# Running sums of k taken by TensorE from the k features; GpSimd's outer products cut from 1152 to 1024 columns

## The chip, the cores and the metric

The kernel runs on one core of one Trainium2 chip. The metric is device time in microseconds, the median of several executions of the same program. Engines are named as the profile names them: PE is TensorE's matmul, PEld its weight load, DVE is VectorE, ACT is ScalarE, POOL is GpSimd, SP is SyncE.

## The reference

The input is 32 x 256 tokens of 128 numbers, in fp32. Three layers follow each other: `x + 0.5 * moe(layernorm(x))`, `x + attention(layernorm(x))`, `x + 0.5 * moe(layernorm(x))`. The first and the last are the same mixture of 8 experts (two for each token) with a shared expert. The one in the middle is a linear attention whose scan runs over the 32 sequences, for each of 256 positions:

```
q, k, v = split((x @ W_attn + b_attn))          # 16 heads of 8
q, k = elu(q) + 1, elu(k) + 1
kv   = kv + k[..., :, None] * v[..., None, :]   # 8 x 8 a head
ksum = ksum + k
y    = (q . kv) / (q . ksum + 1e-6)
out  = y @ W_proj + b_proj
```

With 16 heads, `kv` has 16 x 8 x 8 = 1024 numbers a token and `ksum` has 128.

## The kernel before

Tokens are taken in 16 groups of 512 (`NG`), each of four tiles of 128 (`NJ`). The program has five phases with a barrier between them. Phase 1 is the first MoE's shared expert and routing; phase 2 its experts in blocks of 256 rows. Phase 3 (`streams`) runs, for group m, three things side by side: the attention of group m+1 and m+2, and the shared expert and the routing of the second MoE for group m-1 and m. Phase 4 is the experts of the second MoE, phase 5 the last sum and the store. The change touches phase 3 only.

Each engine has its own instruction list, written out by hand in the order in which it runs; engines wait for each other by counting semaphores. The loop of phase 3 (`streams_of`) has two groups in its body, and three groups ahead of it and four behind it are written out apart.

The attention of a group goes in two halves q = 0, 1 of two tiles a = 0, 1:

- PE makes q, k, v of a tile (`qkv_products`, into banks 3 and 4 of PSUM). ACT takes the exponential and copies v to `val` (L650, L652); DVE makes the features of q and k from them (`features`, `qk`, L1359).
- POOL makes the outer products of a tile (`outer`, L510): `kv` = k times v for each head, with k in `qk` and v in `val`. `val` has 9 columns a head, and the ninth is 1.0 (`VD = HD + 1`, written by `memset` at L547, once), so that one product of 16 x 9 x 8 = 1152 columns (`KVW`) holds k times v and k itself.
- PE turns them into running sums (`running_sums`, L945 and L947). For a = 0 it multiplies the fp32 matrix `upto` (a triangle of ones) by the 1152 columns, in three matmuls of 320, 512 and 320 columns, since a bank of PSUM ends at 512. For a = 1 each of the three is followed by a second one with `ones32` and the columns of a = 0. They lie in `PKV`, columns 192 to 1343 of banks 5 to 7. In the trace each fp32 matmul is two records, each with a weight load of its own.
- DVE multiplies the sums by q (`attend`, L1366, from PSUM to `prod`), adds eight neighbours (L1369, into `num`), and after four tiles divides (`divide`, L1374 to L1378, into `y32`). PE transposes `y32` (L957), ACT and DVE split it in two fp16 parts, and PE projects it.

The waits that the prediction speaks of: PE's `running_sums` waits for POOL's `s_outer` and for DVE's `s_sums_read` (L1366 has read the sums before). DVE's `attend` waits for `s_running_sums`. DVE's `place` (L1219, L1221, `pk` at L1223) gives each token its row in the routing table; ahead of it DVE waits for `s_running_sums` of tile (1, 0). PE's `positions` (L891, L893) waits for the `s_sums_read` of tile (0, 0) of the group after. `deviations` (L1174 to L1192) ends the norms' scale on DVE, and POOL's `outer(m + 1, 1, 0)` waits for it. `combine` (L517) adds the experts' results to X on POOL; `row_low` and `low` (L503) are fp16 remainders; `scatter` (L482, L485) sends 8 indirect DMAs a group from POOL's queue. `keep_warm` (L1055) is nine matmuls that nothing reads.

PE's list for the loop: `gate_up(0)`, `running_sums(0, 1)`, `keep_warm(9)`, `gate_up(1)`, `running_sums(1, 0)`, transposes and qkv of the next half, `running_sums(1, 1)`, transposes, qkv, `down`, `running_sums(0, 0)` of the next group, `logits`, `y_transposes`, `project`, `positions`. POOL's list: `outer(1, 0)`, `low`, `outer(1, 1)`, `combine`, `row_low`, `outer(0, 0)`, `outer(0, 1)`, `scatter`.

## Time and profile before

| | |
|---|---|
| three runs | 1367.43, 1369.38, 1383.91 us |
| median | 1369.38 us |
| profiled execution, first to last instruction | 1240.9 us |
| median less that span | 128.5 us |
| phase 3 (attention) in the profiled execution | about 460 to 947 us |
| busy over the span | PE 80%, DVE 72%, POOL 68%, ACT 54% |

The page gives the profiled execution's span and no time of its own beside it. What lies around the span (median less span) has no instruction of the program in it. A record of the trace has a start, a duration and, in square brackets, how long the engine had been idle before it and what ended that. All times in rows are microseconds from the span's start, except where a column is said to be in ns.

### The profile page before, as it was taken

The page shows a single profiled execution, that of the slowest core. Times are in us where ns is not written, and L with a number is a line of the kernel's source. Part 1 is how long each engine was busy: PE and PEld are TensorE (multiplying, and loading weights), DVE is VectorE, ACT ScalarE, POOL GpSimd, SP SyncE. Part 2 cuts the span into 40 slices and gives each one's busy share as a digit, 9 for nine tenths or more (in the row PEclk, how much of TensorE's full clock was granted, in tenths as well). Part 3 has the DMA queues.
Part 4 walks back from the last instruction along what each step waited for, and adds up shares of the span by engine and source line. Part 5 has one row for each costly group of instructions (what it writes and reads, how often), then busy time and mean ns, then how long its engine had stood idle before and what let it go on. Part 6 is the DMA issues. An engine that isn't in the chain of part 4 may idle for free. (4 is left out here: it accounts for less than half of the span.)

```text
span 1240.9 us, 31979 instructions
## 1 busy us (share of the span) xinstructions
PE 989.7 (80%) x8996; PEld 742.7 (60%) x8997; DVE 896.8 (72%) x2369; ACT 669.6 (54%) x1466; POOL 843.8 (68%) x872
## 2 busy tenths in 40 slices
PE   2657665999999927788888888888864999999940
PEld 1434344899989924455555555555543888899930
DVE  6778784676676745788888888888854666666748
ACT  4556642555555523466665656666331555555545
POOL 4677773777777845467787787778642677777750
PEclk9898996999999968999999999999966999999985
DMA  9411122222222221001111111100003222222229
GB/s 279 108 51 47 52 76 66 78 79 76 78 77 78 68 59 33 17 33 37 34 34 51 34 38 41 41 17 18 23 27 87 74 74 77 78 75 78 73 95 332
DMA packets 68607, 86.62 MB, mean 70 GB/s; under 512 B 13004, under 2 KB 56209, under 8 KB 68558
## 3 DMA queue, kind: packets, MB, share of 16 engines
q1 hardware_dynamic: 51278, 52.15, 14.5%
q0 software_dynamic: 17280, 33.87, 8.3%
q8 instruction: 25, 0.41, 0.1%
q14 instruction: 24, 0.20, 0.1%
HBM read 44.74 MB, written 43.04 MB: 71 GB/s over the span
## 5 line engine op out<-in xcount | busy, mean ns | idle before, releaser
L496 POOL DMA_INDIRECT expert_results<-ey,eidx x284 | 293.3, 1033 | 70.9 <-issue 69.6
L485 POOL DMA_INDIRECT routed_rows<-row,idx x256 | 255.2, 997 | 73.6 <-issue 70.2
L1142 DVE SCALAR_TENSOR_TENSOR ehT<-eh,ehT 128x768 f16<-128x768 f32 x142 | 136.1, 958 | 150.1 <-ACT ehT L688 150.1
L683 ACT ACTIVATE esil<-PSUM 128x768 f32<-128x768 f32 x142 | 115.1, 810 | 230.2 <-PE PSUM L826 224.6
L824 PE MATMUL PSUM<-eT,WGU 128*128 128x256 f16 x852 | 234.3, 275 | 1.4
L825 PE MATMUL PSUM<-eT,WGU 128*128 128x256 f16 x852 | 233.9, 275 | 0.0
L826 PE MATMUL PSUM<-eT,WGU 128*128 128x256 f16 x852 | 233.8, 274 | 0.0
L510 POOL TENSOR_TENSOR space<-qk,val 128x1152 f32<-128x1152 f32 x64 | 138.2, 2171 | 69.5 <-DVE shift L1192 48.7
L824 PE MATMUL PSUM<-WD,ehT 128*128 x852 | 161.0, 220 | 8.3 <-DVE ehT L1142 5.0
L825 PE MATMUL PSUM<-WD,ehT 128*128 x852 | 159.3, 220 | 0.0
L826 PE MATMUL PSUM<-WD,ehT 128*128 x852 | 158.8, 219 | 0.0
L945 PE MATMUL PSUM<-space,upto 128*128 128x320 f32 (+1 forms) x384 | 148.4, 496 | 9.6 <-DVE prod L1366 6.8
L1292 DVE SCALAR_TENSOR_TENSOR eh<-PSUM,esil 128x768 f32<-128x768 f32 x142 | 134.9, 950 | 8.1 <-ACT esil L683 8.1
L494 POOL TENSOR_TENSOR carrier<-ones 128x1 f32<-128x1 f32 x142 | 73.0, 514 | 72.6 <-ACT ey L697 72.6
L688 ACT ACTIVATE ehT<-eh 128x768 f16<-128x768 f32 x142 | 118.6, 835 | 2.5 <-DVE eh L1292 2.5
L945 PEld LDWEIGHTS PSUM<-space,upto 128*128 128x128 f32 x384 | 71.8, 193 | 59.7 <-issue 42.0
L1366 DVE TENSOR_TENSOR prod<-PSUM,qk 128x1152 f32<-128x1152 f32 x64 | 86.3, 1348 | 13.9 <-PE PSUM L947 9.3
L824 PEld LDWEIGHTS PSUM<-eT,WGU 128*128 x852 | 83.7, 98 | 18.8 <-issue 6.8
L824 PEld LDWEIGHTS PSUM<-WD,ehT 128*128 128x128 f16 x852 | 82.9, 97 | 14.3 <-issue 9.7
L1369 DVE TENSOR_REDUCE space<-prod 128x144 f32<-128x1152 f32 x64 | 86.6, 1353 | 5.8
L826 PEld LDWEIGHTS PSUM<-eT,WGU 128*128 x852 | 84.0, 99 | 10.4
L825 PEld LDWEIGHTS PSUM<-eT,WGU 128*128 x852 | 84.1, 99 | 7.3
(197 smaller groups left out, 2300.0 us busy)
## 6 DMA issues: line engine op xcount, KB each, us to landing
xe<-routed_rows SPq DMA_DIRECT2D x142, 130.0 KB, 2.1
space<-expert_results SPq DMA_DIRECT2D x32, 512.0 KB, 3.9
expert_results<-ey,eidx POOLq DMA_INDIRECT x284
X<-in_L_attn_x_dram SPq DMA_DIRECT2D x16, 256.0 KB, 4.6
routed_rows<-row,idx POOLq DMA_INDIRECT x256, 2.3
out_dram<-X SPq DMA_DIRECT2D x16, 256.0 KB, 4.3
routed_rows<-pad_rows SPq DMA_DIRECT2D x24, 130.0 KB
space<-in_L_ffn_Wg_dram SPq DMA_DIRECT2D x1, 1408.0 KB, 9.1
```

Source lines behind the costliest of these rows:

```text
L485: pool.indirect_dma_start(routed, bass.IndirectOffsetOnAxis(ap=idx[u][:, k, j:j + 1], axis=0), row[u][:, j, :], None).then_inc(s_scattered ...
L496: pool.indirect_dma_start(result, bass.IndirectOffsetOnAxis(ap=eidx[u][:, h:h + 1], axis=0), ey[u][:, h, :], None, bounds_check=K * T - 1, ...
L510: pool.tensor_tensor(kv[:, q, a, :].rearrange("p (h j i) -> p h j i", h=HEADS, j=VD), k4, v4, ALU.mult).then_inc(s_outer, 1)
L683: act.activation(esil[u][:, :], PSUM[:, 1536 * u:1536 * u + 768], ACT.Silu, scale=2.0 ** -(SX + SWT)).then_inc(s_block_silu, 1)
L688: act.activation(ehT[u][:, 0, :, :], eh32[u][:, :].rearrange("p (c t) -> p c t", c=NC), ACT.Copy).then_inc(s_block_high, 1)
L824: pe.matmul(dst, a[0], b[0], start=start, stop=False)
L825: pe.matmul(dst, a[0], b[1], start=False, stop=False)
L826: return pe.matmul(dst, a[1], b[0], start=False, stop=stop)
L945: mm = pe.matmul(PKV[:, lo:hi], upto[:, :], kv[:, q, a, lo:hi], start=True, stop=(a == 0))
L1142: return dve.scalar_tensor_tensor(out=dst, in0=src, scalar=float(2 ** scale), in1=high, op0=ALU.mult, op1=ALU.subtract)
L1292: dve.scalar_tensor_tensor(out=eh32[u][:, :], in0=PSUM[:, at:at + NC * BLK], scalar=2.0 ** (SH - SX - SWT), in1=esil[u][:, :], op0=ALU.mul ...
L1369: dve.tensor_reduce(num[:, j, :, :], prod[:, a, :].rearrange("p (h j i) -> p h j i", h=HEADS, j=VD), AX.X, ALU.add)
```

## The change

- `val` has 8 columns a head and is laid out value first: `[HD, HEADS]`, so column j * 16 + h. ACT's copy reads PSUM in steps of 8 fp32 for that and writes without gaps; before, it read without gaps and wrote 8 of each 9. The `memset` of the ones is gone.
- `outer` makes 1024 columns, `kv[j, h, i] = k[h, i] * v[j, h]`.
- `running_sums` first multiplies `upto` (and `ones32`) by the k features themselves, 128 columns of `qk`, then by the two halves of `kv`, 512 columns each. `PKV` is moved to columns 384 to 1535 of banks 5 to 7, so that each piece lies in a bank of its own: 128, 512, 512.
- `attend` reads q as nine copies of a run of 128 instead of 16 x 9 x 8; `num` is value first, with the sum of k in row 0. `divide` reads `num` in that order and writes `y32` with steps of 8 fp32.

```diff
-KVW = HEADS * HD * VD
+KW = HEADS * HD
+KVW = KW * VD
...
-        val = sb("val", [P, 2, 2, HEADS, VD])
-        kv = reused("p (q a w) -> p q a w", q=2, a=2, w=KVW)
-        num = reused("p (j h v) -> p j h v", j=NJ, h=HEADS, v=VD)
+        val = sb("val", [P, 2, 2, HD, HEADS])
+        kv = reused("p (q a w) -> p q a w", q=2, a=2, w=KW * HD)
+        num = reused("p (j v h) -> p j v h", j=NJ, v=VD, h=HEADS)
...
-        KV0 = (3 * 512 - KVW) // 2
-        PKV = bank(5, 3)[:, KV0:KV0 + KVW]
+        PKV = bank(5, 3)[:, 3 * 512 - KVW:3 * 512]
...
-                k4 = qk[:, q, a, D:2 * D].rearrange("p (h j i) -> p h j i", h=HEADS, j=1).to_broadcast([P, HEADS, VD, HD])
-                v4 = val[:, q, a, :, :].rearrange("p h (j i) -> p h j i", i=1).to_broadcast([P, HEADS, VD, HD])
-                pool.tensor_tensor(kv[:, q, a, :].rearrange("p (h j i) -> p h j i", h=HEADS, j=VD), k4, v4, ALU.mult
+                k4 = qk[:, q, a, D:2 * D].rearrange("p (j h i) -> p j h i", j=1, h=HEADS).to_broadcast([P, HD, HEADS, HD])
+                v4 = val[:, q, a, :, :].rearrange("p j (h i) -> p j h i", i=1).to_broadcast([P, HD, HEADS, HD])
+                pool.tensor_tensor(kv[:, q, a, :].rearrange("p (j h i) -> p j h i", j=HD, h=HEADS), k4, v4, ALU.mult
                                    ).then_inc(s_outer, 1)
...
-                    for q in range(2):
-                        pool.memset(val[:, q, :, :, HD:VD], 1.0)
...
-                    last = act.activation(val[:, q, a, :, 0:HD], PG[a][:, 2 * D:3 * D].rearrange("p (h j) -> p h j", h=HEADS),
+                    last = act.activation(val[:, q, a, :, :], PG[a][:, 2 * D:3 * D].rearrange("p (h j) -> p j h", h=HEADS),
...
-                for lo, hi in ((0, 512 - KV0), (512 - KV0, 1024 - KV0), (1024 - KV0, KVW)):
-                    mm = pe.matmul(PKV[:, lo:hi], upto[:, :], kv[:, q, a, lo:hi], start=True, stop=(a == 0))
+                pe.matmul(PKV[:, 0:KW], upto[:, :], qk[:, q, a, D:2 * D], start=True, stop=(a == 0))
+                if a:
+                    pe.matmul(PKV[:, 0:KW], ones32[:, :], qk[:, q, 0, D:2 * D], start=False, stop=True)
+                for lo in (0, 512):
+                    sums = PKV[:, KW + lo:KW + lo + 512]
+                    mm = pe.matmul(sums, upto[:, :], kv[:, q, a, lo:lo + 512], start=True, stop=(a == 0))
                     if a:
-                        mm = pe.matmul(PKV[:, lo:hi], ones32[:, :], kv[:, q, 0, lo:hi], start=False, stop=True)
+                        mm = pe.matmul(sums, ones32[:, :], kv[:, q, 0, lo:lo + 512], start=False, stop=True)
...
-                q4 = qk[:, q, a, 0:D].rearrange("p (h j i) -> p h j i", h=HEADS, j=1).to_broadcast([P, HEADS, VD, HD])
+                q3 = qk[:, q, a, 0:D].rearrange("p (v c) -> p v c", v=1).to_broadcast([P, VD, KW])
...
-                dve.tensor_tensor(y32[:, :, :].rearrange("p j (h i) -> p j h i", h=HEADS), num[:, :, :, 0:HD],
-                                  rden[:, :, :].rearrange("p j (h i) -> p j h i", i=1).to_broadcast([P, NJ, HEADS, HD]),
+                dve.tensor_tensor(y32[:, :, :].rearrange("p j (h i) -> p j i h", h=HEADS), num[:, :, 1:VD, :],
+                                  rden[:, :, :].rearrange("p j (i h) -> p j i h", i=1).to_broadcast([P, NJ, HD, HEADS]),
                                   ALU.mult).then_inc(s_y, 1)
```

## Rows read from the trace of the kernel before

**Rows 1.** Busy time by stretch, two groups of the loop (busy us by engine, count):

```profile
core 0: us, PE busy (x) PEld busy (x) DVE busy (x) ACT busy (x) POOL busy (x), PEclk, DMA share, GB/s
620.61:647.99 27.38, 24.01 (x151) 14.97 (x149) 23.64 (x65) 17.61 (x39) 22.37 (x18) 1.00 0.12 39
647.99:675.37 27.38, 24.02 (x147) 14.73 (x145) 24.14 (x64) 17.39 (x39) 20.87 (x18) 1.00 0.11 39
```

**Rows 2.** Records of DVE in order of time, two groups:

```profile
620.61 0.19 DVE L1219 TENSOR_TENSOR posb<-PSUM,base 128x32 f32<-128x32 f32 x1 [1.06 <-PE PSUM L945]
620.95 0.49 DVE L1223 TENSOR_TENSOR pk<-pick,posb 128x64 f32<-128x64 f32 x1
...
627.59 1.36 DVE L1366 TENSOR_TENSOR prod<-PSUM,qk 128x1152 f32<-128x1152 f32 x1 [0.18 <-PE PSUM L947]
...
635.84 1.35 DVE L1366 TENSOR_TENSOR prod<-PSUM,qk 128x1152 f32<-128x1152 f32 x1
...
647.99 0.19 DVE L1219 TENSOR_TENSOR posb<-PSUM,base 128x32 f32<-128x32 f32 x1 [1.26 <-PE PSUM L945]
...
648.33 1.13 DVE L1223 TENSOR_TENSOR pk<-pick,posb 128x64 f32<-128x64 f32 x1
...
655.40 1.33 DVE L1366 TENSOR_TENSOR prod<-PSUM,qk 128x1152 f32<-128x1152 f32 x1
...
663.72 1.34 DVE L1366 TENSOR_TENSOR prod<-PSUM,qk 128x1152 f32<-128x1152 f32 x1
...
675.37 0.19 DVE L1219 TENSOR_TENSOR posb<-PSUM,base 128x32 f32<-128x32 f32 x1 [1.06 <-PE PSUM L945]
```

**Rows 3.** Records of PE in order of time, from positions to the sums:

```profile
637.33 0.18 PE L891 MATMUL PSUM<-chosen,before 128*128 128x32 f16 x1 [0.51 <-DVE prod L1366]
...
643.12 1.51 PE L1055 MATMUL PSUM<-SGW,ident 128*128 128x352 f16 x9
...
645.76 2.10 PE L945 MATMUL PSUM<-space,upto 128*128 128x320 f32 x6
```

**Rows 4.** Records of POOL in order of time, same two groups:

```profile
619.19 2.18 POOL L510 TENSOR_TENSOR space<-qk,val 128x1152 f32<-128x1152 f32 x1
621.32 1.27 POOL L517 TENSOR_TENSOR X<-X,space 128x512 f32 x1
...
642.49 2.17 POOL L510 TENSOR_TENSOR space<-qk,val 128x1152 f32<-128x1152 f32 x1 [1.29 <-DVE shift L1192]
644.87 1.16 POOL L503 TENSOR_TENSOR xa<-xn,xa 128x512 f16<-128x512 f32 x1 [0.21 <-ACT xa L641]
645.98 2.17 POOL L510 TENSOR_TENSOR space<-qk,val 128x1152 f32<-128x1152 f32 x1
648.11 1.26 POOL L517 TENSOR_TENSOR X<-X,space 128x512 f32 x1
...
654.33 4.30 POOL L510 TENSOR_TENSOR space<-qk,val 128x1152 f32<-128x1152 f32 x2 [1.44 <-DVE qk L1359]
```

**Rows 5.** Groups by line and shape, 500 to 880 us (busy us, mean ns | idle before):

```profile
L510 POOL TENSOR_TENSOR space<-qk,val 128x1152 f32<-128x1152 f32 x56 | 121.0, 2171 | 53.1 <-DVE shift L1192 40.2 <-DVE qk L1359 12.3
L945 PEld LDWEIGHTS PSUM<-space,upto 128*128 128x128 f32 x336 | 61.9, 190 | 45.5 <-issue 30.6 <-POOL space L510 2.2
L482 POOL TENSOR_TENSOR ticket<-ones 128x1 f32<-128x1 f32 x13 | 2.5, 191 | 0.0
L1198 DVE TENSOR_REDUCE lg<-PSUM 128x32 f32<-128x64 f32 x14 | 3.0, 212 | 0.0
L1226 DVE TENSOR_REDUCE idx<-pk 128x8 uint32<-128x64 f32 x13 | 2.9, 220 | 1.4
L1378 DVE TENSOR_TENSOR space<-space,rden 128x512 f32<-128x512 f32 x14 | 9.7, 696 | 1.0
L652 ACT ACTIVATE val<-PSUM 128x128 f32<-128x128 f32 x56 | 12.2, 274 | 0.0
```

**Rows 6.** fp32 transposes of 128 columns, weight loads and matmuls:

```profile
632.83 0.42 PEld L957 LDWEIGHTS PSUM<-ident,space 128*128 128x128 f32 x4
632.83 0.66 PE L957 MATMUL PSUM<-ident,space 128*128 128x128 f32 x4
```

**Rows 7.** Records of DVE and PE ahead of the loop, behind POOL's products:

```profile
477.50 1.36 DVE L1366 TENSOR_TENSOR prod<-PSUM,qk 128x1152 f32<-128x1152 f32 x1 [0.61 <-PE PSUM L945]
...
485.39 2.20 PE L945 MATMUL PSUM<-space,upto 128*128 128x320 f32 x6 [0.93 <-POOL space L510]
...
510.39 2.20 PE L945 MATMUL PSUM<-space,upto 128*128 128x320 f32 x6 [1.82 <-POOL space L510]
```

**Rows 8.** Records of DVE's pk in other groups:

```profile
539.41 0.22 DVE L1223 TENSOR_TENSOR pk<-pick,posb 128x64 f32<-128x64 f32 x1
...
593.71 1.06 DVE L1223 TENSOR_TENSOR pk<-pick,posb 128x64 f32<-128x64 f32 x1
...
812.60 1.13 DVE L1223 TENSOR_TENSOR pk<-pick,posb 128x64 f32<-128x64 f32 x1
```

More of the change, by code:

```diff
@@ L1364, in attend @@
                 dve.wait_ge(s_running_sums, m * NJ + (j + 1))
[L1365 to L1367 removed]
+                q3 = qk[:, q, a, 0:D].rearrange("p (v c) -> p v c", v=1).to_broadcast([P, VD, KW])
+                dve.tensor_tensor(prod[:, a, :].rearrange("p (v c) -> p v c", v=VD),
+                                  PKV[:, :].rearrange("p (v c) -> p v c", v=VD), q3, ALU.mult).then_inc(s_sums_read, 1)
                 dve.drain()
[L1369 removed]
+                dve.tensor_reduce(num[:, j, :, :], prod[:, a, :].rearrange("p (v h i) -> p v h i", v=VD, h=HEADS),
                                   AX.X, ALU.add)
@@ L1373, in divide @@
                 dve.drain()
-                dve.tensor_scalar(rden[:, :, :], num[:, :, :, HD], EPS_DEN * 4.0 ** SF, None, ALU.add)
+                dve.tensor_scalar(rden[:, :, :], num[:, :, 0, :], EPS_DEN * 4.0 ** SF, None, ALU.add)
                 dve.drain()
```

3 lines of the change are left out of this document (removed).

## The prediction

> **What bounds the kernel now.** The change touches only the attention phase, so I left the chain of work that ended last aside (it shows the experts and their indirect DMAs) and read the phase as a loop. First, busy time by stretch over one group and the next [rows 1]: both take 27.38 us; PE is busy 24.0 of them, DVE 23.6 to 24.1, POOL 20.9 to 22.4. Nobody is full, PE and DVE are nearly so, and POOL, the engine that the change relieves, has 5 to 6 us to spare. A busy share says nothing about order, so next came the records of each engine in order of time. The reader is to look for the points where one engine waits for another and where that other is itself not waiting.
>
> The loop closes like this. PE finishes the sums of tile (1, 0), and DVE, which had been idle for 1.06 or 1.26 us, starts `place` at 620.61 and 647.99 [rows 2]. From there DVE works almost without a gap until it has multiplied the sums of tile (0, 0) of the next group, at 635.84 and 663.72 [rows 2]. PE waited for that, with `positions` at 637.33 [rows 3], and from there runs without a pause that another engine causes through `gate_up`, the sums of (0, 1), `keep_warm`, `gate_up` and the sums of (1, 0), which start at 645.76 and let DVE go at 647.99 [rows 2, 3]. So of 27.38 us some 10.7 are PE's (637.33 to 647.99) and 16.7 are DVE's. POOL is in neither part. Its product (1, 0) ends at 644.66, 1.1 us ahead of the PE record that needs it; its product (1, 1) ends at 648.15, when DVE, in `place`, has yet to read the sums ahead of it; its first product of the next group ends at about 656.5, halfway into the pair that starts at 654.33, and those sums come last in PE's list [rows 3, 4]. In front of the first product POOL stands idle for 1.29 us, waiting for DVE [rows 4].
>
> There is one place where POOL's length does reach the loop. DVE's `pk` (L1223), 64 elements with both inputs in SBUF, takes 0.22 us where nothing is in its way [rows 8], 0.49 us at 620.95 and 1.13 us at 648.33 [rows 2]. At 620.95 it ends at 621.44, when POOL's product does (621.37); at 648.33 it has missed the end of the product (648.15) and ends at 649.46, when POOL's `combine` does (648.11 + 1.26 = 649.37) [rows 2, 4]. So `pk` stands still while POOL works, and the two groups of the loop body alternate: in the first it is caught by the end of the product, in the second by `combine`.
>
> **The change part by part.**
>
> *POOL's products.* From 1152 to 1024 columns, 64 times. One takes 2171 ns, and a product of one column 191 ns [rows 5], so a column costs (2171 - 191) / 1151 = 1.72 ns and 128 columns 0.22 us. Bounds: proportional to columns it is 0.24; against `combine`, 512 columns in 1.26 us [rows 4], it is (2.17 - 1.26) / 640 x 128 = 0.18. Together 64 x 0.22 = 14 us of POOL, nearly all of it in waits that POOL has already. In the loop `low` (L503) still starts when ACT has its input (it waited 0.21 us for it [rows 4]), so product (1, 1) starts where it did, and ends 0.22 earlier.
>
> *What that gives in the loop.* `combine` starts and ends 0.22 earlier, and so does a `pk` that it holds. Inside the loop's rhythm there are five groups in which `pk` took over 1 us, every second one, from 593.71 to 812.60 [rows 2, 8]. Does DVE pass it on? Counted from `place`, its multiply for tile (1, 1) starts at 7.41 us (655.40) in such a group without a wait, and at 6.98 us (627.59) in the other with one of 0.18 us for PE [rows 2]. So there are 0.43 us to be had before PE's order stops it: the 0.22 pass, 5 x 0.22 = 1.1 us. In the other kind of group `pk` gets 0.22 shorter too, but PE is what DVE waits for a little later, so that is worth nothing. It is still free of `combine` there: it starts at 620.95, the product would end at 621.15, and `pk` at 539.41 took 0.22 us although a product and `combine` met at that time.
>
> *What it gives ahead of the loop.* In the first groups PE waits for the product itself: 0.93 and 1.82 us, and once DVE waits 0.61 us behind such sums [rows 7]. Three times 0.22 is 0.7 us. Behind the loop PE waits for DVE and ACT, not for POOL: nothing.
>
> *PE's matmuls.* 320 + 512 + 320 = 128 + 512 + 512 = 1152 columns, as many matmuls, as many records. What is new is the short one, two records of 128 columns, four where a = 1. The question is whether a weight load hides under one. An fp32 load of `upto` is recorded at 190 ns [rows 5]. The stream of a record can be read from the sums of (1, 0): 2 x 1152 = 2304 columns in 2.10 us with the last one's tail [rows 3], at most 0.91 ns a column, 117 ns for 128. The nearest rows are the fp32 transposes: four records of 128 columns take 0.66 us with the last one's tail, and their four loads, each recorded at some 140 ns, take 0.42 us [rows 6], so one follows the other every (0.42 - 0.14) / 3 = 0.09 us. A load longer than the stream that covers it thus did not set the pace, and I take 0 us for the short records. The bound on the other side is 190 - 93 = 97 ns for each.
>
> *DVE's multiply and reduce.* As many elements from as many bytes in one run: 0, no row of another shape. The wait for `s_outer` stays ahead of the k matmul, so PE starts no earlier by its not needing POOL. PE now reads `qk` itself; DVE rewrites it only behind the `attend` that waits for those sums, so no wait is added and nothing new is queued behind one.
>
> *The layout.* ACT's copy of v reads PSUM with steps of 32 bytes (274 ns, 64 in the phase), and `divide`'s last step writes `y32` with steps of 32 bytes (696 ns, one a group) [rows 5]. DVE's L1198 reads 64 numbers of PSUM with just such steps in 212 ns, and L1226, of as many with no gap, takes 220 [rows 5]: steps cost nothing in a read. For writes no row shows it; I take 0, and as a bound a rate half as high. The `memset` of the ones ran while POOL waited for ACT: 0.
>
> *The sum.* -1.1 - 0.7 = -1.8 us against the profiled span of 1240.9. The 128.5 us between that and the median hold no instruction, so the same difference goes onto the median: 1369.4 - 1.8 = 1367.6 us.
>
> **A rule that speaks against it.** The Trainium skill (Advanced Engine Details and Errata, Memory Cachelines) says that SBUF works in lines of 16 bytes and wants two hits on a line for full speed, and PSUM in lines of 8 bytes. By it both accesses of the new layout, with one hit a line, would pay, which is rival B. The trace disagrees for DVE's read of PSUM (L1198) and shows nothing for the write.
>
> **The rivals.**
>
> A. *The weight load shows under the short records (slower).* Place: sums of (0, 1) with four short records and of (1, 0) with two, both in PE's part of the loop: 6 x 97 = 0.58 us a group, 8 us over 14 groups. From there it gets worse at a point: `pk` in the first kind of group is 0.2 us ahead of the product's end, so as soon as PE's part is longer by about 0.3 us it falls into `combine` and takes 1.1 instead of 0.26 us, of which 0.18 vanish in the wait for PE: 6 x 0.7 = 4 us. Together 12 - 1.8, some 1380 us. For it: the recorded 190 ns. Against it: rows 6.
>
> B. *The strided accesses cost (slower).* 512 numbers at half the rate: 0.53 us a group, in DVE's part: 8.5 us. ACT's two copies of the second half at 2 x 0.11, just ahead of the DVE record that waits for them: 16 x 0.22 = 3.5. Together 12 - 1.8, some 1380 us.
>
> C. *The gain does not arrive*, since `pk` is caught otherwise or the product has another fixed part: 1369.4 us.
>
> D. *POOL sets the pace after all*, and all of 64 x 0.24 = 15.4 us comes: 1354 us. Against it stands the slack of 1.1 us at the product with the least of it.
>
> **How the numbers follow.** The forecast gets 0.69, C 0.16, A 0.06, B 0.07, D 0.02. A measurement of this kernel tells a change from none at about 2%, 27 us, and none of the cases reaches that; 0.02 and 0.03 remain for what I have not thought of. The range goes from 1362, where the price of a product is larger and more `pk` are freed, to 1378, just below the full A and B; A, B and D left out are about 0.15.
>
> **What the profile after would show.** L510 at 1.95 us (D and C: whether POOL only waits longer for DVE's `shift`); short records of L942 and L944 following each other every 0.11 us and six records of the sums of (1, 0) still spanning 2.1 us (A: 2.3, and 4.3 instead of 3.9 for those of (0, 1)); `pk` alternating 0.26 and 0.9 us (A: all over 1); L1378 at 0.70 us and the copy of v at 0.27 us (B: 1.2 and 0.38); two groups at 54.5 us instead of 54.76. The prediction would be wrong if the phase's length moved by more than 3 us while these hold.

## The result, and the profile after

| | before | after |
|---|---|---|
| four runs each | 1367.43 to 1383.91 us | 1391.83 to 1397.13 us |
| median | 1373.35 us | 1394.34 us |
| ratio (95% interval) | | 1.016 (1.0112 to 1.0208) |

The change made the kernel slower, by about 1.6%; the forecast was 1.8 us less. Times are compared between ordinary executions of a kernel; the profiles of the runs `after_again`, `after_filler_between` and `before_filler_first_moe` are of somewhat slower ones, so of them I use the counts, and lengths with care. Rows of the page of after (span; busy us, share and instructions by engine; two rows of the costliest groups):

```profile
span 1390.1 us, 31978 instructions
PE 1059.0 (76%) x8996; PEld 746.0 (54%) x8997; DVE 907.4 (65%) x2369; ACT 676.8 (49%) x1466; POOL 813.9 (59%) x870
L681 ACT ACTIVATE esil<-PSUM 128x768 f32<-128x768 f32 x142 | 115.0, 810 | 164.2 <-PE PSUM L824 94.4
L510 POOL TENSOR_TENSOR space<-qk,val 128x1024 f32<-128x1024 f32 x64 | 125.3, 1969 | 100.8 <-DVE shift L1194 85.2
```

This execution took 1391.83 us, so its span is its time less 1.7 us. The same holds for a second profile of the kernel before, taken on another chip with the first experiments (1396.03 us median, run `before_again`):

```profile
span 1392.6 us, 31979 instructions
PE 1055.5 (76%) x8996; PEld 755.2 (54%) x8997; DVE 902.3 (65%) x2369; ACT 676.8 (49%) x1466; POOL 826.5 (59%) x872
```

So nothing of note lies around the span. The first profile has no time beside its 1240.9 us; since every later profile is 1.7 to 1.8 us short of its time, I take it for an exceptionally quick execution. Split into phases (us; the first up to the experts' first `esil`, the others from the first to the last record of one line of each):

| | first MoE, routing | its experts | attention | second MoE's experts |
|---|---|---|---|---|
| before, first profile | 207 | 231.2 | 426.2 | 232.9 |
| before, second profile | 254 | 276.5 | 427.4 | 283.5 |
| after | 253 | 269.7 | 447.7 | 272.1 |

The phases that the change doesn't touch were 40 to 50 us quicker in the first profile. The attention phase was not, so the rows of it that the prediction used are good ones; after added 20 us there.

What the short products and the rest of the change cost by themselves, from the groups by line and shape of the attention phase (busy us, mean ns | idle before), first after:

```profile
L510 POOL TENSOR_TENSOR space<-qk,val 128x1024 f32<-128x1024 f32 x63 | 123.3, 1969 | 93.9 <-DVE shift L1194 85.2 <-DVE qk L1361 7.9
L1368 DVE TENSOR_TENSOR prod<-PSUM,qk 128x1152 f32<-128x1152 f32 x64 | 86.4, 1350 | 9.1 <-PE PSUM L949 5.0 <-PE PSUM L947 3.9
L1380 DVE TENSOR_TENSOR space<-space,rden 128x512 f32<-128x512 f32 x16 | 17.4, 1087 | 1.2
L650 ACT ACTIVATE val<-PSUM 128x128 f32<-128x128 f32 x62 | 13.5, 273 | 0.0
L1225 DVE TENSOR_TENSOR pk<-pick,posb 128x64 f32<-128x64 f32 x14 | 10.4, 746 | 0.0
```

and the second profile of before:

```profile
L1366 DVE TENSOR_TENSOR prod<-PSUM,qk 128x1152 f32<-128x1152 f32 x64 | 86.1, 1346 | 8.8 <-PE PSUM L945 3.8 <-PE PSUM L947 3.2 <-issue 1.7
L1223 DVE TENSOR_TENSOR pk<-pick,posb 128x64 f32<-128x64 f32 x15 | 13.1, 876 | 0.0
L1378 DVE TENSOR_TENSOR space<-space,rden 128x512 f32<-128x512 f32 x16 | 11.1, 693 | 1.2
```

Against [rows 5], the product fell from 2171 to 1969 ns and POOL only waited longer for DVE's `shift` (85 us in all; in the attention phase 78.1, against 43.4 in the second profile of before). ACT's copy of v with steps stayed at 273 ns. The divide's last step, which now writes with 32-byte steps, went from 693 to 1087 ns: 0.39 us in each of 16 groups, 6.3 us. That is a third of the 20.

The rest is in a wait. ACT's `words` copies `which` into the row (L626 before, L624 after) behind a wait for `s_projected`, which PE signals with the last matmul of `project`; then ACT writes the residual that DVE's norm waits for. Waits by pair (us, times, longest), after and then before:

```profile
ACT row L624 <- remote: 52.6, 12, 6.5
```

```profile
ACT row L626 <- remote: 5.8, 1, 5.8
```

"remote" is what the trace puts down when the semaphore changed and no record that could have changed it ends near that time. One group of after, records of POOL, DVE, PE and ACT in order:

```profile
721.57 1.01 POOL L485 DMA_INDIRECT routed_rows<-row,idx  x1
722.88 0.96 POOL L485 DMA_INDIRECT routed_rows<-row,idx  x1 [0.30 <-issue]
723.30 1.09 DVE L1380 TENSOR_TENSOR space<-space,rden 128x512 f32<-128x512 f32 x1
724.14 0.96 POOL L485 DMA_INDIRECT routed_rows<-row,idx  x1 [0.31 <-issue]
...
728.18 0.22 PE L824 MATMUL PSUM<-PW,yaT 128*128 128x128 f16 x1
...
730.83 0.38 PE L942 MATMUL PSUM<-qk,upto 128*128 128x128 f32 x2
731.05 0.39 PE L944 MATMUL PSUM<-qk,ones 128*128 128x128 f32 x2
731.28 1.02 PE L947 MATMUL PSUM<-space,upto 128*128 128x512 f32 x2
...
733.01 0.21 ACT L624 ACTIVATE row<-which 128x4 f32<-128x4 uint32 x1 [6.51 <-remote]
733.88 0.87 DVE L1166 BATCH_NORM_STATS2 stats<-X 128x6 f32 x4 [3.67 <-ACT X L673]
737.83 1.97 POOL L510 TENSOR_TENSOR space<-qk,val 128x1024 f32<-128x1024 f32 x1 [6.40 <-DVE shift L1194]
738.69 0.41 PE L822 MATMUL PSUM<-xT,SGW 128*88 128x512 f16 x1 [2.47 <-ACT ssil L606]
```

The projection's last matmul ends at 728.40, and ACT starts at 733.01, 4.6 us late. PE itself went on at once with `positions`, `gate_up` and the sums, until it waited 2.47 us for ACT.

The trace also has the time at which each semaphore changed, and this tells where the 4.6 us are. `s_projected` changed at 732.99, 0.02 us before ACT starts, so ACT did not sleep through a signal that was there. Three other signals that PE gave meanwhile, one by `positions` at 729.18 and two by `gate_up` at 730.35 and 731.00, changed their semaphores at 733.05, 733.11 and 733.16, right behind it. DVE's signal of 728.76, given in the same stretch, arrived at 728.78. So all of PE's signals wait, in their order, and those of DVE don't. It is the same in 78 of the 80 late groups counted below (in two the record of the change is missing): ACT starts 0.02 us after the change, and no signal that PE gave in the meantime arrives before it.

The same place in the second profile of before:

```profile
699.33 1.01 POOL L485 DMA_INDIRECT routed_rows<-row,idx  x1
700.27 0.69 DVE L1378 TENSOR_TENSOR space<-space,rden 128x512 f32<-128x512 f32 x1
700.64 1.16 POOL L485 DMA_INDIRECT routed_rows<-row,idx  x1 [0.30 <-issue]
702.10 0.96 POOL L485 DMA_INDIRECT routed_rows<-row,idx  x1 [0.30 <-issue]
...
705.13 0.21 ACT L626 ACTIVATE row<-which 128x4 f32<-128x4 uint32 x1 [1.96 <-PE PSUM L826]
```

Here the projection ends at 705.02 and ACT starts 0.11 us later. I call a release late when ACT starts more than 1 us behind that last record. In the 13 groups in whose projection a scatter is under way, the second profile of before had 1 late release and after had 13. A release late by 2.07 us goes with a group of 28.4 to 28.9 us, one late by 4.61 with 31.2, where 27.4 + 0.39 = 27.8 would be the group without: about 1.2 us of the lateness is covered, the rest counts. Taken from one projection's end to the next it comes out closely: each of the eleven intervals between late groups of after is the lateness at its start plus 26.6 to 26.9 us. Summed over the groups that is 17.9 us in after and 2.8 in before; with the divide's 6.3 us it makes 21 of the 20.3 us that the phase grew. That is what they take in this execution; what a kernel without them wins is less, as the experiments show.

The reader should also see one difference between the two sets of rows: in before the scatter's second issue falls into DVE's divide step and is held (1.16 us instead of 0.96); in after it begins before that step (722.88 against 723.30) and isn't.

### The profile page after: what moved, and what is told of

Same layout as the page of the kernel before. It is cut to its first block and busy times, and to the rows that moved or that the text cites. A ratio compares the mean times of both kernels' runs of the same rounds, so it can differ in the third digit from the quotient of the medians.

```text
span 1390.1 us, 31978 instructions
## 1 busy us (share of the span) xinstructions
PE 1059.0 (76%) x8996; PEld 746.0 (54%) x8997; DVE 907.4 (65%) x2369; ACT 676.8 (49%) x1466; POOL 813.9 (59%) x870
## 5 line engine op out<-in xcount | busy, mean ns | idle before, releaser
L496 POOL DMA_INDIRECT expert_results<-ey,eidx x284 | 314.8, 1109 | 97.4 <-issue 97.1
L822 PE MATMUL PSUM<-WD,ehT 128*128 x852 | 169.2, 220 | 28.9 <-ACT ey L695 11.3
L510 POOL TENSOR_TENSOR space<-qk,val 128x1024 f32<-128x1024 f32 x64 | 125.3, 1969 | 100.8 <-DVE shift L1194 85.2
L823 PE MATMUL PSUM<-WD,ehT 128*128 x852 | 163.8, 220 | 4.8 <-issue 4.8
L824 PE MATMUL PSUM<-WD,ehT 128*128 x852 | 163.5, 219 | 4.3 <-issue 4.2
L947 PE MATMUL PSUM<-space,upto 128*128 128x512 f32 x256 | 126.7, 597 | 0.0
L494 POOL TENSOR_TENSOR carrier<-ones 128x1 f32<-128x1 f32 x142 | 37.0, 261 | 143.7 <-ACT ey L695 141.6
L822 PEld LDWEIGHTS PSUM<-WD,ehT 128*128 128x128 f16 x852 | 82.7, 97 | 54.6 <-issue 50.5
L822 PEld LDWEIGHTS PSUM<-eT,WGU 128*128 x852 | 83.6, 98 | 28.6 <-issue 18.4
L694 ACT ACTIVATE eidx<-places 128x2 uint32 (+1 forms) x142 | 28.7, 202 | 137.6 <-PE PSUM L824 94.8
L823 PEld LDWEIGHTS PSUM<-WD,ehT 128*128 128x128 f16 x852 | 82.6, 97 | 14.4 <-issue 5.6
L824 PEld LDWEIGHTS PSUM<-eT,WGU 128*128 x852 | 83.9, 98 | 10.9 <-issue 0.3
```

What stands on the lines that cost most here:

```text
L496: pool.indirect_dma_start(result, bass.IndirectOffsetOnAxis(ap=eidx[u][:, h:h + 1], axis=0), ey[u][:, h, :], None, bounds_check=K * T - 1, ...
L510: pool.tensor_tensor(kv[:, q, a, :].rearrange("p (j h i) -> p j h i", j=HD, h=HEADS), k4, v4, ALU.mult).then_inc(s_outer, 1)
L822: pe.matmul(dst, a[0], b[0], start=start, stop=False)
L823: pe.matmul(dst, a[0], b[1], start=False, stop=False)
L824: return pe.matmul(dst, a[1], b[0], start=False, stop=stop)
L947: mm = pe.matmul(sums, upto[:, :], kv[:, q, a, lo:lo + 512], start=True, stop=(a == 0))
```

## The experiments

Ratios are to the kernel before on the same chip; the parts ran on different chips, and the kernel after itself had 1.016 on one and 1.024 on another, so ratios of different tables are compared loosely. "Late" counts the groups as above, out of 13.

**1. Both kernels again, and the divide's layout.** `before_again` and `after_again` are the two kernels unchanged.

> The kernel before, unchanged, to have its profile and time beside those of the changed one on one chip. The first profile of it has a span of 1240.9 us, while its timed runs are at 1367 to 1384 us and the changed kernel's profile has 1390.1 in a run of 1391.8, so hardly anything lies around the span. Theory 1 (the first profile caught a quicker execution; the difference of 21 us between the kernels is all in the attention phase): ratio 1.00, a span about 2 us below its time, the attention phase (first to last multiply by q, 426 us in the first profile) at 426 to 436 us. Theory 2 (the kernels differ in the phases that the change does not touch too): its routing and expert phases are shorter than those of the changed kernel by several us in the same state.

> The changed kernel, unchanged. Both theories: ratio 1.012 to 1.02. Theory 1: the attention phase, first to last multiply by q, is 445 to 450 us again, some 20 more than before's; the other phases within 3 us of before's. Theory 2: the other phases differ by 5 us or more.

`y_gapless` is after with the steps on the reading side:

```diff
-dve.tensor_tensor(y32[:, :, :].rearrange("p j (h i) -> p j i h", h=HEADS), num[:, :, 1:VD, :],
+dve.tensor_tensor(y32[:, :, :].rearrange("p j (h i) -> p j h i", h=HEADS), num[:, :, 1:VD, :].rearrange("p j i h -> p j h i"),
```

> The changed kernel with one step undone: the last step of divide writes y32 without gaps and reads num and the reciprocals with steps instead. Theory W (the write with steps of 32 bytes is what costs): L1380 falls from 1.09 to about 0.70 us, 16 times, and the time falls by 6 us or more (0.39 us stand in DVE's chain of each group), to a ratio of about 1.010 if the rest of the 21 us has another cause, and to 1.00 if the longer step also upset the rhythm of the loop. Rival (a step costs on either side): L1380 stays at 1.09 and nothing changes. Rival R (the rhythm of waits, not this step, holds the 21 us): L1380 falls and the ratio stays above 1.012.

`before_y_steps` is before with that step's output (and its operands' order) as in after:

```diff
-dve.tensor_tensor(y32[:, :, :].rearrange("p j (h i) -> p j h i", h=HEADS), num[:, :, :, 0:HD],
+dve.tensor_tensor(y32[:, :, :].rearrange("p j (h i) -> p j i h", h=HEADS), num[:, :, :, 0:HD].rearrange("p j h i -> p j i h"),
```

> The kernel before with this one step added alone: divide writes y32 with steps of 8 fp32 as the changed kernel does (the values are the same), all else as before. Theory W: L1378 rises from 0.70 to 1.09 us and the kernel gets slower by 6 us, ratio 1.005. If the longer step upsets the rhythm of the loop: 1.015. Rival R: L1378 rises and the time stays within 2 us.

| | median us | ratio (interval) | late | attention, us |
|---|---|---|---|---|
| before_again | 1396.03 | 1.0018 (0.9978 to 1.0059) | 1 | 427.4 |
| after_again | 1436.69 | 1.0236 (1.016 to 1.0312) | 13 | 477.1 |
| y_gapless | 1428.32 | 1.0244 (1.0189 to 1.0299) | 13 | 465.6 |
| before_y_steps | 1413.79 | 1.0128 (1.0068 to 1.0189) | 4 | 447.0 |

The result holds on this chip and is larger there. Reading with steps of 64 bytes is hardly cheaper than writing with 32, so `y_gapless` mends nothing:

```profile
L1380 DVE TENSOR_TENSOR space<-space,rden 128x512 f32<-128x512 f32 x15 | 15.2, 1014 | 1.1
```

`before_y_steps` adds 6.3 us of DVE but 18 us of time (a ratio of 1.0128). It also has groups of both kinds, two of them here. First one in time:

```profile
779.61 1.09 DVE L1378 TENSOR_TENSOR space<-space,rden 128x512 f32<-128x512 f32 x1
779.69 1.78 POOL L485 DMA_INDIRECT routed_rows<-row,idx  x1 [0.30 <-issue]
...
784.80 0.21 ACT L626 ACTIVATE row<-which 128x4 f32<-128x4 uint32 x1 [1.92 <-PE PSUM L826]
...
808.98 0.96 POOL L485 DMA_INDIRECT routed_rows<-row,idx  x1 [0.30 <-issue]
809.01 1.09 DVE L1378 TENSOR_TENSOR space<-space,rden 128x512 f32<-128x512 f32 x1
...
818.39 0.21 ACT L626 ACTIVATE row<-which 128x4 f32<-128x4 uint32 x1 [6.10 <-remote]
```

An issue that begins 0.08 us after the divide step's start is held for 0.8 us and the release is in time; one that begins 0.03 us before it goes through, and the release is late.

**2. One part at a time.** `short_products` is before with the product over 1024 of its 1152 columns, the sum of k being replaced by a constant:

```diff
-k4 = qk[...].rearrange("p (h j i) -> p h j i", h=HEADS, j=1).to_broadcast([P, HEADS, VD, HD])
+k4 = qk[...].rearrange("p (h j i) -> p h j i", h=HEADS, j=1).to_broadcast([P, HEADS, HD, HD])
```

> The kernel before with the shorter GpSimd products alone: each covers 1024 of the 1152 columns, in the old order; the ninth column of each head in kv is filled once with a constant, so the sum of k is left out (a count of tokens stands in its place). PE, DVE and ACT do exactly what they did. Theory S (ACT's wait for the projection, L626, is let go some 2 to 5 us late in groups where the waits of the other engines fall so, and what POOL does and when shifts that): L510 takes 1.97 us, the number of such late groups goes from 1 in the profile of before to several, attention phase 435 us or more, ratio 1.005 to 1.02. Rival P (the sum of the prediction: less work on POOL can only help): attention phase 425 to 427 us, ratio 0.998 to 1.00, at most one late group.

`after_long_products` is after with products of 1152 columns again, of which 128 are not read:

```diff
-val = sb("val", [P, 2, 2, HD, HEADS])
+val = sb("val", [P, 2, 2, VD, HEADS])
...
-... .to_broadcast([P, HD, HEADS, HD])
+... .to_broadcast([P, VD, HEADS, HD])
```

> The changed kernel with the GpSimd products back at 1152 columns (the last 128, k itself, are made and not read), so that POOL's timing is that of before; all else as changed. Theory S: what stays is the kernel before with the slower last step of divide, so 4 late groups or so, attention phase 447 us as with that step alone, ratio 1.010 to 1.015, well under the 1.024 of the changed kernel on the same chip. Rival L (the late groups come from the new layout or the k matmuls, not from POOL's timing): 12 or 13 late groups and 1.02 to 1.025 again.

`before_dve_delay` is before with a sum that nobody reads ahead of the divide's last step:

```diff
+dve.tensor_reduce(scratch[:, :], bias_f[:, 0:240].rearrange("p (a b) -> p a b", b=8), AX.X, ALU.add)
 dve.tensor_tensor(y32[:, :, :]...
```

> The kernel before with 0.4 us more on DVE ahead of the last step of divide: a sum over 240 constants that nothing reads. No access pattern is changed. Theory S: as with the slow write (0.39 us), 3 to 6 late groups, attention phase 440 to 450 us, ratio 1.010 to 1.015. Rival B' (writing with steps disturbs something more than its own 0.39 us, such as ACT or PE): at most one late group, attention phase 427 + 6 = 433 us, ratio 1.004.

`after_no_scatter` is after without the 128 indirect DMAs of the second MoE, short memsets in their place (its experts work on the first MoE's rows):

```diff
+if ffn[0]:
+    pool.memset(scratch[:, u, k, j, :], 1.0).then_inc(s_filled_row[u], 1)
+else:
     pool.indirect_dma_start(routed, ...)
```

> The changed kernel with the second MoE's 128 indirect DMAs of the attention phase left out (the experts of phase 4 then work on the rows of the first MoE); short memsets stand in their place in POOL's list. Theory D (the late releases of ACT come from the DMAs that POOL issues at that time, or from their completions): no late group, L624 starts 0.3 us behind the last projection matmul in all, attention phase about 430 us. Rival E (they come from the engines' own timing): several late groups remain, attention phase above 440 us.

| | median us | ratio (interval) | late | attention, us |
|---|---|---|---|---|
| short_products | 1406.76 | 1.0271 (1.0222 to 1.0321) | 13 | 460.8 |
| after_long_products | 1381.32 | 1.0078 (1.004 to 1.0117) | 3 | 437.5 |
| before_dve_delay | 1391.01 | 1.0132 (1.0063 to 1.0202) | 7 | 448.3 |
| after_no_scatter | 1384.65 | 1.0099 (1.0061 to 1.0137) | 0 | 444.8 |

The short products alone, which take 13 us of work away and add none, make the kernel 2.7% slower; with long products after loses at least half its deficit. `before_dve_delay` costs as much as `before_y_steps` (1.013) with no access pattern changed, so the write with steps acts through the 0.4 us that it takes and nothing else needs to be assumed. That is the heart of it. The mechanism can be read in a group of `short_products`: the second issue begins 0.39 us before the divide step and is not held.

```profile
723.90 0.96 POOL L485 DMA_INDIRECT routed_rows<-row,idx  x1 [0.30 <-issue]
724.29 0.69 DVE L1379 TENSOR_TENSOR space<-space,rden 128x512 f32<-128x512 f32 x1
...
732.50 0.21 ACT L627 ACTIVATE row<-which 128x4 f32<-128x4 uint32 x1 [5.31 <-remote]
```

In before it began 0.37 us after the step's start (700.64 against 700.27); the two products ahead of the scatter are 2 x 0.20 = 0.40 us shorter, and that alone is enough to bring it to the step's start. The records show a shift of 0.4 to 0.8 us; in the group here DVE's L1375 also took 0.42 us instead of 0.22, which puts the divide step later. Over nine profiles with the scatter in its old place and no filler (those of parts 1 and 2 but `after_no_scatter`, the first one of after, and `after_few_words` below), 37 groups had an issue held ahead of the projection's end and 80 had none. Of the 37 no release was late; of the 80 every one was. The first kind had begun five issues by 0.3 us behind the projection's end, the second six, so these profiles can't tell the missing break from the sixth issue. Four more can (`short_products_filler`, `after_filler_1200` and `before_filler_all` of part 3, `before_filler_first_moe` of part 5). Late releases in all thirteen together, by the issues begun at that moment:

| begun | run unbroken | one issue held |
|---|---|---|
| six | 85 of 85 | |
| five | 15 of 17 | 0 of 45 |
| four | 1 of 6 | 0 of 16 |

With five begun the break decides. With four an unbroken run does little: the one that counts as late is so by 1.03 us.

"In time" holds for this one signal only. By the times at which the semaphores changed, PE's next signals, of `positions` and `gate_up` 0.8 to 2.9 us behind the projection's end, were late by 2 to 5 us in 35 of the 37 groups too, in all 13 of the second profile of before among them. There ACT waits for `gate_up` instead, in the attention phase

```profile
ACT ssil L608 <- remote: 15.5, 12, 3.3
```

and the loop has room for that. So before has the lateness as well, a moment later: what the shorter products do is to move its onset, by less than 1 us, ahead of the one signal of these that the loop cannot wait for. In `after_no_scatter`, `after_filler_between` and `before_filler_between_all` none of these signals is late, and none in the first profile of before.

Without the scatter no release is late, so its issues are needed for it. The phase of that run is still 17 us longer than before's, 6.3 of it the divide. My expectation of about 430 us for it was wrong. Two of its groups (busy us by engine, count, then granted clock, DMA share, GB/s):

```profile
649.88:677.58 27.70, 23.96 (x151) 14.03 (x149) 23.75 (x64) 17.60 (x39) 13.05 (x18) 1.00 0.06 20
...
733.06:762.53 29.47, 25.65 (x147) 14.74 (x145) 24.64 (x65) 17.40 (x39) 14.99 (x18) 0.94 0.05 18
```

The first is the 27.8 us of the sum above. In the other, PE runs at 1.2 instead of 2.4 GHz for a part of the time and the group is 1.8 us longer. Four of the first seven whole groups have clock 1.00 and three 0.94; what lets the clock fall in these I have not settled. The second profile of before has 1.00 over the phase; those with late releases have 0.96 to 0.99, but `after_no_scatter` and `after_filler_between`, which have none, 0.97 and 0.98 too, so it does not come with the late releases. Nor is it a part of what I count as lateness: of the eleven intervals of after that are the lateness plus 26.6 to 26.9 us, four have a clock of 0.94 and seven 1.00. It costs where no release is late, and so takes back a part of what their absence gives.

**3. Moving the scatter, and its bytes.** `short_products_filler` and `after_filler_1200` put a memset ahead of each attention scatter:

```diff
 if settle:
+    pool.memset(filler[:, :], 1.0)
+    pool.drain()
     scatter(m + (NG - 1), 1 - u)
```

> This is the kernel with the short products (kernel before, GpSimd's product over 1024 of 1152 columns, sum of k left out of the computation), with one GpSimd write of 420 columns (about 0.45 us) put ahead of each scatter of the attention phase, so that the scatter starts as long after the products as in the kernel before. Theory S (where the scatter's issues fall beside the projection's end decides whether ScalarE is released late): of 14 groups at most 4 have the late release, against 13 without the filler, and the ratio falls from 1.027 to 1.000 to 1.008. Rival (the shorter product itself does it, in whatever way): 10 or more late groups, ratio 1.02 or more.

> The kernel after, with one GpSimd write of 1200 columns (about 1.25 us, the length of one issue) ahead of each scatter of the attention phase. Theory S: the sixth issue moves from 0.4 us before the projection's end to about 0.9 us behind it, where the groups of the kernel before that are in time have it; at most 4 of 14 releases are late, the attention phase falls from 448 us to 430 to 437 us, and the ratio to the kernel before is 0.998 to 1.006. Rival (GpSimd's place doesn't matter, or later issues only move the trouble): 10 or more late releases, ratio 1.015 or more.

`before_filler_all` has the 420-column memset behind the `ticket` of every scatter.

> The kernel before with one GpSimd write of 420 columns (0.45 us) in each of the 32 scatters, those of the first MoE too. In the attention phase it moves the issues further behind the projection's end: no late release or one, nothing to gain (at most 4 us). In the first phase, of 254 us where the quick execution took 207, it is a trial: if the place of the issues decides there too, the phase changes by 10 us or more in either direction; if not, it grows by 0 to 7 us (16 x 0.45) and the ratio is 1.000 to 1.005.

`after_few_words`, in the second MoE's scatter:

```diff
-pool.indirect_dma_start(routed, ..., row[u][:, j, :], None)
+pool.indirect_dma_start(routed_few, ..., row[u][:, j, 0:4], None)
```

> The kernel after, with the second MoE's scatter sending only 4 of the 130 words of each row, into a tensor that nobody reads (so the second MoE's experts work on the first MoE's rows). GpSimd issues as many indirect DMAs in the same places. Theory T (the rows' traffic holds the release back): the late releases go, as they did without the scatter: 0 to 3 of 14, ratio 1.004 to 1.010. Theory I (GpSimd's issuing holds it back): 10 to 14 late releases, ratio 1.012 to 1.02.

| | median us | ratio (interval) | late | attention, us |
|---|---|---|---|---|
| short_products_filler | 1405.63 | 1.0093 (1.0046 to 1.014) | 12 | 447.2 |
| after_filler_1200 | 1402.73 | 1.0058 (1.0019 to 1.0098) | 0 | 442.2 |
| before_filler_all | 1412.9 | 1.0142 (1.0058 to 1.0226) | 4 | 439.1 |
| after_few_words | 1431.65 | 1.0285 (1.0194 to 1.0376) | 13 | 471.1 |

Bytes are not it: with 4 words of 130 all 13 stay late. The issues are: without any there was none late. For the short filler my expectation was wrong, 12 stayed late, if by less (2.0 to 3.4 us, five issues begun, against 2.3 to 5.2 and six in `short_products`). With its drain it moved the scatter by 1.1 to 1.2 us and not by 0.45, so that the first issue begins 0.3 to 0.5 us before the divide step and the second 0.8 to 1.0 us after its start: again none is held, but in one group of 13. The long one moved it by 1.6 to 1.9 us and so brought the *first* issue into the divide step (0.12 to 0.22 us behind its start) in 11 groups of 13, and none was late. Its attention phase was still 442 us, not the 430 to 437 expected. Of the loss some moved on: DVE's product of the shared hidden half now waits in its turn, in the attention phase

```profile
DVE PSUM L1236 <- remote: 17.5, 11, 2.0
```

where the second profile of before has no such wait for PE at this line. For `before_filler_all` my expectation was wrong as well: 4 late instead of none or one, and a first phase 14 us longer.

**4. The scatter ahead of the products, and in halves.** POOL's list with the scatter before `outer(0, 0)` and `outer(0, 1)`, in both kernels, and in after with four issues before them and four behind:

```diff
+if settle:
+    scatter(m + (NG - 1), 1 - u)
 if ready:
     outer(m + 2, 0, 0)
     outer(m + 2, 0, 1)
-if settle:
-    scatter(m + (NG - 1), 1 - u)
```

> The kernel before, with the scatter of a step placed in GpSimd's list ahead of the two products for the next group instead of behind them (attention phase only). TensorE reads those products some 14 us later, so the 10.2 us that they wait should cost nothing by themselves; the issues end at about the projection's end. If a release is late only because issues are under way at it: 0 or 1 late, attention phase 424 to 430 us, ratio 0.995 to 1.003. If the loss moves to whichever of TensorE's signals now falls among the issues (the turned rows for ScalarE, the logits for VectorE): other waits marked remote appear, attention phase 435 us or more, ratio 1.008 or more.

> The same move in the kernel after. Theory that the issues' place at the projection's end decides: 0 to 3 late releases of 14 against 13, attention phase 430 to 437 us (the divide's last step keeps its 6 us), ratio to the kernel before 0.999 to 1.007. Rival (the loss moves to other signals): attention phase 442 us or more, ratio 1.012 or more.

> The kernel after with four of the scatter's eight issues ahead of the two products and four behind them. Issues are still under way at the projection's end, the fifth starting some 1.5 to 2 us ahead of it, with four gone long before. If an issue under way is enough: 8 or more late releases, ratio 1.012 or more. If it takes more than five of them in one row: 0 to 3 late, ratio below 1.008.

| | median us | ratio (interval) | late | attention, us |
|---|---|---|---|---|
| before_scatter_first | 1501.99 | 1.0758 (1.0646 to 1.087) | 0 | 539.7 |
| after_scatter_first | 1501.34 | 1.0762 (1.0656 to 1.0868) | 0 | 539.2 |
| after_split_scatter | 1434.45 | 1.0295 (1.0191 to 1.0399) | 0 | 467.8 |

I had misread the slack: the sums of (0, 0), which I took to be read 14 us later, wait for the moved products, as these records of `before_scatter_first` show, together with a late release at another wait for PE, DVE's L1241. That one has 13 waits, 48.8 us in all; the second profile of before has one of 1.9 us.

```profile
721.66 0.69 DVE L1241 SCALAR_TENSOR_TENSOR X<-PSUM,X 128x512 f32 x1 [3.97 <-remote]
722.11 1.44 PE L945 MATMUL PSUM<-space,upto 128*128 128x320 f32 x2 [6.89 <-POOL space L510]
```

So the ratios measure mostly the wait for the products (in `after_split_scatter`, 21.5 us of PE's in the phase), and my expectations of them were wrong. What they do tell: the late release is no property of ACT or of `s_projected`; it goes where a PE signal falls behind a run of issues. And in runs of four, with products between, there was none, neither at ACT's wait nor at DVE's.

**5. A gap inside the run.** A memset of 600 columns between the fourth and the fifth issue; in the attention phase of after (as here), in all 32 scatters of before (`if k:`), and in before in the first MoE's 16 alone (`if k and not ffn[0]:`):

```diff
 for k in range(K):
+    if k and ffn[0]:
+        pool.memset(filler[:, :], 1.0)
+        pool.drain()
     for j in range(NJ):
         pool.indirect_dma_start(routed, ...
```

> The kernel after with one GpSimd write of 600 columns (about 0.6 us) between the fourth and the fifth issue of each scatter of the attention phase; the scatter's start and the products stay where they are. If an unbroken run of more than four issues is what holds the release back: at most 3 of 14 late, attention phase 430 to 438 us, ratio 0.999 to 1.007. If it is the time from the scatter's start to the projection's end (6.4 to 6.8 us in the late groups): 10 or more late, ratio 1.014 or more.

> The kernel before with the same 0.6 us write between the fourth and the fifth issue of all 32 scatters, those of the first MoE too. If the run's length decides: the first phase falls from 252 to 256 us by 10 us or more, attention 427 us or less, ratio below 0.995, a kernel faster than both. If not: the first phase stays or grows by up to 10 us (16 x 0.6) and the ratio is 1.000 to 1.012.

> The kernel before with the 0.6 us write between the fourth and the fifth issue of the 16 scatters of the first MoE alone. If the run's length decides: first phase 232 to 240 us as in the last run, attention 427 to 432 us with 0 or 1 late release, ratio 0.984 to 0.992, faster than both kernels. If the first phase's gain was chance: 250 us or more and a ratio of 0.998 to 1.003.

| | median us | ratio (interval) | late | routing of the first MoE, us | attention, us |
|---|---|---|---|---|---|
| after_filler_between | 1377.91 | 1.0071 (1.0022 to 1.012) | 0 | 253 | 436.0 |
| before_filler_between_all | 1364.6 | 0.9965 (0.9923 to 1.0008) | 0 | 236 | 438.8 |
| before_filler_first_moe | 1386.4 | 0.992 (0.9877 to 0.9963) | 5 | 241 | 450.4 |

One group of `after_filler_between`. The issues begin as in after and none is held, yet the release is in time; the memset and what follows it leave 2.3 us between two issues.

```profile
782.31 1.00 POOL L489 DMA_INDIRECT routed_rows<-row,idx  x1 [0.30 <-issue]
783.61 0.96 POOL L489 DMA_INDIRECT routed_rows<-row,idx  x1 [0.30 <-issue]
784.57 0.62 POOL L486 MEMSET filler<- 128x600 f32 x1
786.61 0.21 ACT L628 ACTIVATE row<-which 128x4 f32<-128x4 uint32 x1 [1.89 <-PE PSUM L828]
786.83 0.96 POOL L489 DMA_INDIRECT routed_rows<-row,idx  x1 [1.64 <-issue]
```

Eight of its groups take 27.6 to 27.7 us, which is the 27.8 of the sum; a ratio of 1.007 is 9.7 us, of which the divide is 6.3. In the first MoE the same gap takes 13 and 18 us off a phase that had 250 to 256 in all runs that left its scatter alone (`before_filler_all`, with the memset ahead of the run, had 269). Its waits by pair fell from

```profile
ACT shT L615 <- remote: 38.3, 10, 4.6
DVE posb L1219 <- remote: 34.0, 10, 4.9
```

in the second profile of before to these in `before_filler_first_moe`:

```profile
ACT shT L619 <- remote: 17.6, 6, 4.6
DVE posb L1223 <- remote: 16.9, 5, 4.4
```

That kernel beats before by 0.8% (after it did not meet on one chip), with none of the change under study in it. Its attention phase, untouched, had 5 late releases in the profiled execution against 1 in before's, so it gives some of the gain back.

The gap is not free. In `before_filler_between_all` the attention phase took 438.8 us against 427.4 and my 427 or less, without one late release, and the ratio did not get below 0.995. POOL's waits for `shift` ahead of its first product fell from 11 (43.4 us) to 2 (12.1 us): the scatter is now so long that the product starts right behind its last issue, and POOL, which was in neither part of the loop, has become one. A gap pays where releases are late, in the first phase, and costs where they aren't.

## Why the prediction was wrong

*The attention loop and its engines: right as far as it went.* PE's and DVE's parts close the loop, POOL is in neither (rival D is out: 13 us less of POOL's work gave no gain, and its waits for `shift` grew).

*POOL's products, 0.22 us each, 14 us: right* (0.20, 13 us). *`pk` freed:* it did become shorter, 746 ns in the mean against 876. Of a gain from it nothing can be seen under the rest.

*PE's short records at 0: right.* L942, L944 and L947 start 0.22 us apart with two records each, 0.11 us a record, and rival A's weight load of 190 ns never shows: the sums of a tile a = 0 span 2.16 us against 2.15 in the second profile of before, those of a = 1 4.04 against 4.03.

*The layout at 0: wrong in one of two places.* ACT's read of PSUM with steps costs nothing (273 ns), DVE's write with steps costs 0.39 us of 0.69; I had extrapolated from reads of 64 numbers, bounded it at 0.53 and taken the wrong end. The Trainium skill's rule (Advanced Engine Details and Errata, Memory Cachelines), which I had weighed and put at 0.07 as rival B, agrees with the measured DVE step in both directions, writing at 32 bytes and reading at 64, but not with ACT's read of PSUM (where it speaks of matmuls). This is 6.3 us, a third of the loss, so B was half right in its mechanism and far from enough in size.

*The step that failed is the sum's premise that a shorter POOL product can only help or do nothing.* I followed the products forward to who waits for them, and not to what POOL does next: the scatter of eight indirect DMAs starts 0.4 to 0.8 us sooner relative to DVE. Its second issue then begins before DVE's divide step instead of 0.37 us into it, is no longer held there, and eight issues go out in one unbroken run. In before PE's signals behind the projection's end are late, and their readers have the time; now the lateness takes in the projection's own. PE's signal at the projection's end, given when six of them have begun, changes its semaphore 1.8 to 4.6 us late, and DVE's norm, POOL's products and PE's next `gate_up` stand behind it. Shown by: `short_products` (2.7% slower by that alone), `after_long_products` (3 late instead of 13), `after_no_scatter` (0), and `after_filler_between` (0, with a first half of the issues that begins where after's does). The term that the sum put at nothing measured 15 us in the phase (17.9 less the 2.8 of before), of which the kernels without late releases won 3 to 12 back (444.8 to 436.0 us against 447.7).

*"The 128.5 us hold no instruction, so the difference goes onto the median": wrong.* A span is its execution's time less 1.7 us. The first profile was of an execution in which no wait is marked remote, in any phase. I had put two executions of a different kind into one line of arithmetic, and with it hid the very effect that the change then set off. In that quick execution two groups had unbroken runs, and their releases were in time: why an execution can be free of late releases altogether stays open.

*My range* took in the divide's cost but no such mechanism. To "what I have not thought of" I gave 0.05, and not even that had room, since the forecast and the four rivals already add up to 1.00.

## What to carry to other kernels

Compare a profiled execution's span with the runs' times first. A gap of 9% is not "around the span" until a row shows it there; ask for a second profile, and look for waits that no record explains. When an engine off the critical path gets faster, follow its list to the next thing that it issues, DMAs above all, and ask what that now falls beside. A row of indirect DMAs that runs without a break beside a signal of TensorE deserves a gap, and here a gap made by 0.6 us of work was worth 13 to 18 us in one phase and cost 11 us in another, where hardly a release had been late: put it in where the late ones are, and measure each place.

## What the runs showed of the hardware

- A semaphore wait on a PE signal was released 1.6 to 5.4 us after PE's last matmul in 85 of 85 groups where six indirect DMA issues of GpSimd (0.96 us every 1.27 us) had begun without a break, in 15 of 17 with five, and in 0 of 61 where one had been held; there it was the next signals, up to 2.9 us behind, that were late (in 35 of 37 groups looked at). The exception is the quick execution of 1240.9 us, with two such groups of six and both in time. It met ACT and DVE alike and did not depend on the bytes (4 or 130 words a row). PE itself was not held. Its semaphores changed late, all signals of that time one behind the other, some 0.06 us apart, while DVE's arrived at once (in 74 of the 80 groups; in 6 its record is missing). So the delay lies on the way of PE's signals and not in the waiting engine; why a run of issues causes it, none of the runs tells.
- An indirect DMA issue that begins 0.06 to 0.39 us into a DVE step from SBUF to SBUF of 512 fp32 numbers takes 1.16 to 1.80 us instead of 0.96: it ends some 0.2 us behind DVE's next step, the residual add. One that begins before the step, or up to 0.03 us into it, is not held, and one that begins 0.8 us or more into a step of 1.09 (724.14 against 723.30 above) ends no sooner than there anyway and takes its 0.96. Here this hold kept the projection's signal ahead of the late ones.
- That DVE step takes 0.69 us without gaps, 1.09 writing with steps of 32 bytes, 1.01 reading with steps of 64. ACT's copy of 128 fp32 from PSUM takes 273 ns with steps of 32 bytes and 274 without.
- The profiled spans of one program were 1392.6 us and, once, 1240.9.
